# The end of the front of a two-layer macaron kernel: batch 0's score maxima in 1024-column units, ScalarE issuing two steps' transfers, and another order on SyncE's queue

## The reference, cut to what matters

```python
x = x + 0.5 * _L0_ffn_ref(_layernorm(x), W1, b1, W2, b2)
...
scores = jnp.einsum('bhqd,bhkd->bhqk', q, k) * scale
scores = jnp.where(causal, scores, -jnp.inf)
y_ar = jnp.einsum('bhqk,bhkd->bhqd', jax.nn.softmax(scores, axis=-1), v)
```

## Time and profile before

| what | value |
|---|---|
| time, median of 3 runs | 645.68 us (642.53 to 649.96) |
| profiled execution | 643.67 us |
| its span, first to last instruction | 641.9 us |
| PE busy | 521.5 us (81%) |
| DVE busy | 359.4 us (56%) |
| ACT busy | 197.0 us (31%) |
| POOL busy | 189.0 us (29%) |
| mean granted PE clock | 0.953 |

### The profile page before, as it was taken

How to read it: one execution, slowest core, us unless ns; L and a number is a source line. 1 busy time by engine, 2 the same in 40 slices (tenths; PEclk the granted TensorE clock), 3 DMA queues, 4 the chain that set the end, 5 groups by cost and what they waited for, 6 DMA issues and landing times.

```text
span 641.9 us, 10406 instructions
## 1 busy us (share of the span) xinstructions
PE 521.5 (81%) x3895; PEld 326.7 (51%) x3895; DVE 359.4 (56%) x942; ACT 197.0 (31%) x282; POOL 189.0 (29%) x228
## 2 busy tenths in 40 slices
PE   0788767999899989989877897894888878788893
PEld 0555333444544463445345773693345556663693
DVE  4753666466766767685044564132587888853131
ACT  0455331453154324424633450120223221110120
POOL 5676463010011102011110346654321212322163
PEclk9996798999999999999998997997998999988998
DMA  7317978732353244225269912323275455211320
GB/s 245 147 34 219 283 234 279 199 115 61 91 148 83 93 87 143 59 59 114 78 129 141 290 59 100 96 87 91 91 221 161 112 163 147 79 34 36 95 64 9
DMA packets 73666, 79.85 MB, mean 124 GB/s; under 512 B 10946, under 2 KB 50499, under 8 KB 73360
## 3 DMA queue, kind: packets, MB, share of 16 engines
q1 hardware_dynamic: 71056, 73.61, 41.4%
q0 software_dynamic: 2560, 5.58, 2.5%
HBM read 44.07 MB, written 35.72 MB: 124 GB/s over the span
## 4 chain that ended last, share of the span: by engine, by line
PE 49%; DVE 20%; issue 7%; DMA 6%; ACT 6%; POOL 5%; SPq 5%; POOLq 0%; DVEq 0%; ACTq 0%
PE ps_accum L1428 21%; PE ps_pair L1428 18%; PE ps_turn L1428 6%; DMA sb_ring<-sb_qs 3%; PE ps_turn L1436 2%; DVE sb_work L1178 2%; SPq L356 2%; POOL sb_rstd L569 2%; DVE sb_work L1323 2%; DVE sb_stats L1001 2%; DVE sb_mpart L1104 2%; SPq L350 1%; POOL xe_scr L589 1%; DMA sb_cols<-in_bias_cols 1%; PE ps_turn L1593 1%
## 5 line engine op out<-in xcount | busy, mean ns | idle before, releaser
L846 ACT ACTIVATE sb_work<-ps_pair 128x1024 f32<-128x1024 f32 x80 | 80.3, 1026 | 52.6 <-PE ps_pair L1428 51.8
L1104 DVE TENSOR_REDUCE sb_mpart<-ps_turn 128x4 f32<-128x512 f32 x80 | 55.0, 688 | 28.2 <-PE ps_turn L1428 28.1
L1428 PE MATMUL ps_pair<-sb_ring,sb_xsets 128*128 128x512 f32 x160 | 62.3, 465 | 6.7 <-ACT sb_work L846 3.5
L1104 DVE TENSOR_REDUCE sb_mpart<-ps_accum 128x4 f32<-128x512 f32 x80 | 55.0, 688 | 19.1 <-PE ps_accum L1428 18.3
L1428 PE MATMUL ps_pair<-sb_ident_bf,sb_ones_bf 128*128 128x512 bf16 x189 | 52.5, 437 | 12.1 <-DMA sb_x<-y_scr 7.8
L1428 PE MATMUL ps_accum<-sb_work,sb_v_aug 128*32 128x128 f32 (+3 forms) x768 | 53.9, 393 | 0.3 <-ACT sb_work L846 0.3
L1428 PE MATMUL ps_turn<-sb_ring,sb_m_sets 128*128 128x512 f32 x80 | 38.1, 477 | 9.4 <-DVE sb_mpart L1104 9.2
L567 POOL TENSOR_SCALAR sb_ve<-sb_mv 128x4 f32<-128x4 f32 x24 | 5.5, 228 | 133.5 <-DVE sb_mv L1004 126.9
L1428 PE MATMUL ps_accum<-sb_ring,sb_m_sets 128*128 128x512 f32 x80 | 40.6, 507 | 4.4 <-DVE sb_mpart L1104 3.8
L650 POOL TENSOR_TENSOR sb_e_pad<-sb_v_next,sb_y_ar 128x128 f32<-128x128 f32 x16 | 7.4, 460 | 122.8 <-DVE sb_y_ar L1148 122.8
L1428 PEld LDWEIGHTS ps_pair<-sb_ident_bf,sb_ones_bf 128*128 128x128 bf16 x189 | 20.4, 110 | 37.5 <-issue 13.2
(11 more groups left out here) (251 smaller groups left out, 991.3 us busy)
## 6 DMA issues: line engine op xcount, KB each, us to landing
sb_expert_rows<-xe_scr SPq DMA_DIRECT2D x16, 258.0 KB, 2.8
sb_m_sets<-q_scr SPq DMA_DIRECT2D x16, 256.0 KB
sb_xsets<-k_scr SPq DMA_DIRECT2D x16, 256.0 KB
sb_ka_stk<-mk_scr SPq DMA_DIRECT2D x4, 1024.0 KB
xe_scr<-sb_cst SPq DMA_DIRECT2D x4, 1024.0 KB, 12.8
sb_mw<-in_mw SPq DMA_DIRECT2D x16, 256.0 KB, 6.1
sb_ka_stk<-mk_scr SPq DMA_DIRECT2D x8, 512.0 KB
q_scr<-sb_qs SPq DMA_DIRECT2D x12, 256.0 KB, 3.4
```

Source lines behind the costliest of these rows:

```text
L846: act.activation(banks[:, 2 * i:2 * i + 2], pair[u % 2][:], ACT.Exp, scale=SCALE).then_inc(s["exp_done"], 1)
L1104: dve.tensor_reduce(mpart[:, m // NPAIR, m % NPAIR, :], max_banks[m % 2][:].rearrange("p (h k) -> p h k", h=HL), AX.X, ALU.max).then_inc(s ...
L1428: return pe.matmul(dst, lhsT, rhs, start=start, stop=stop, skip_group_check=True)
```

## The change

It has five parts.

1. The PSUM banks are declared anew: the two narrow banks become the halves of one double bank `max_pair`, and `wide_banks` are `pair[0]` and `max_pair`. `turn[1]` and `accum[1]` are now names for those halves.
2. Units 12 to 39 of batch 0 are done two at a time: `wide_scores` on PE fills both halves and signals once, `wide_maxima` on DVE reduces 1024 columns in one instruction. DVE's casts for batch 3 stand behind unit 17, no more behind unit 15.
3. ACT issues batch 0's first exponentials' set itself (`first_exp_set`), then loads the table of Exp, then does `max_t`, then issues the first row of maxima.
4. SP no longer issues those six transfers. Its order is now: `keep_features(3)`, batch 1's first maxima set, the second exponentials' set, the values, the second row.
5. `stay_awake` before the attention has 8 matmuls for 12.

```diff
--- before.py
+++ after.py
@@ -129,9 +129,11 @@
 
 
         pair = [psum(f"pair{i}", [P, 2, 512]) for i in range(2)]
-        accum = [psum(f"accum{i}", [P, 512]) for i in range(2)]
-        turn = [psum(f"turn{i}", [P, 512]) for i in range(2)]
-        max_banks = [turn[1], accum[1]]
+        max_pair = psum("max_pair", [P, 2, 512])
+        max_banks = [max_pair[:, i] for i in range(2)]
+        wide_banks = [pair[0][:], max_pair[:]]
+        accum = [psum("accum0", [P, 512]), max_banks[1]]
+        turn = [psum("turn0", [P, 512]), max_banks[0]]
 
         cst = sb("cst", [P, CONSTS.shape[1]])
 
@@ -438,17 +440,15 @@
             next_max_set(0, 1)
             keep_softmax(3)
             keep_features(3)
-            hold(sp, s["ffn_h"], NF * B)
-            for hs in range(2):
-                load_exp_set(0, hs)
-            hold(sp, s["v_kept"], 16 * B)
-            load_values(0)
             for kept in ("q_kept", "k_kept"):
                 hold(sp, s[kept], 48 * B)
             next_max_set(0, 2)
+            hold(sp, s["ffn_h"], NF * B)
+            load_exp_set(0, 1)
+            hold(sp, s["v_kept"], 16 * B)
+            load_values(0)
             hold(sp, s["max_t_evac"], 1)
-            for hs in range(2):
-                max_row(0, hs)
+            max_row(0, 1)
             next_max_set(0, 3)
             for kept in ("mq_kept", "mk_kept"):
                 hold(sp, s[kept], 48 * B)
@@ -829,6 +829,16 @@
                     act.wait_ge(s["q_kept"], 48 * B)
                 act.copy(mT, turn[1][0:H, :]).then_inc(s["max_t_evac"], 1)
 
+            def first_exp_set():
+
+                act.wait_ge(s["pad_zero"], 80)
+                act.wait_ge(s["q_kept"], 48)
+                act.wait_ge(s["k_kept"], 48)
+                for hl in range(HL):
+                    act.dma_start(ring[VW * hl:VW * hl + 3 * HD, 0, hl].bitcast(F32),
+                                  head_rows(q_scr, 0, hl, 3 * HD)).then_inc(s["xset0"], 16)
+                act.dma_start(x_sets[:, 0].bitcast(F32), set_rows(k_scr, 0, 0)).then_inc(s["xset0"], 16)
+
             def answers_out(b, hs):
 
                 act.wait_ge(s["pv_mm"], STEPS * b + NT * hs + NT)
@@ -877,8 +887,11 @@
             projections(B - 1)
             features(B - 1)
             keys_in_tokens(B - 1)
+            first_exp_set()
+            ready(ACT.Exp)
             max_t(0)
-            ready(ACT.Exp)
+            act.wait_ge(s["max_t_evac"], 1)
+            act.dma_start(ring[3 * HD:3 * HD + 1, 0].bitcast(F32), mT[0:HL].bitcast(F32)).then_inc(s["xset0"], 16)
             act.wait_ge(s["mq_kept"], 48 * B)
             act.wait_ge(s["mk_kept"], 48 * B)
             for b in range(B):
@@ -1104,6 +1117,15 @@
                     dve.tensor_reduce(mpart[:, m // NPAIR, m % NPAIR, :],
                                       max_banks[m % 2][:].rearrange("p (h k) -> p h k", h=HL),
                                       AX.X, ALU.max).then_inc(s["smax_red"], 1)
+
+            def wide_maxima(first, last):
+
+                for m in range(first, last, 2):
+                    hs, i = m // NPAIR, m % NPAIR
+                    dve.wait_ge(s["smax_mm"], m + 2)
+                    dve.tensor_reduce(mpart[:, hs, i:i + 2, :].rearrange("p i h -> p (i h)"),
+                                      wide_banks[m // 2 % 2].rearrange("p i (h k) -> p (i h) k", h=HL),
+                                      AX.X, ALU.max).then_inc(s["smax_red"], 2)
 
             def max_of_tiles(b):
 
@@ -1245,11 +1267,11 @@
             normalise(norm_first(3), x[3], xn_first[3], norm_first(3) % 2)
             for b in range(1, B):
                 before_attention(b)
-            maxima(0, 12, 16)
+            wide_maxima(12, 18)
             split(B - 1, 0)
             split(B - 1, 1)
             query_features(B - 1)
-            maxima(0, 16, NM)
+            wide_maxima(18, NM)
             max_of_tiles(0)
             for b in range(B):
                 attention(b)
@@ -1552,6 +1574,21 @@
                         last = mm(dst, ident_bf[:], bc(add_q_bf[:], HL), start=False)
                     last.then_inc(s["smax_mm"], 1)
 
+            def wide_scores(first, last_m):
+
+                for m in range(first, last_m, 2):
+                    hs = m // NPAIR
+                    if m % NPAIR == 0:
+                        pe.wait_ge(s[f"mset{hs % 2}"], 80 * (hs // 2 + 1))
+                    pe.wait_ge(s["smax_red"], m - 2)
+                    for a in range(2):
+                        qt, kt = MAX_PAIRS[m % NPAIR + a]
+                        dst = wide_banks[m // 2 % 2][:, a]
+                        last = mm(dst, tile(m_sets[:, hs % 2], qt), ring[:, 2 + hs % 2, :, kt * P:(kt + 1) * P], stop=qt != kt)
+                        if qt == kt:
+                            last = mm(dst, ident_bf[:], bc(add_q_bf[:], HL), start=False)
+                    last.then_inc(s["smax_mm"], 2)
+
             def max_turn(b):
                 pe.wait_ge(s["smax_red"], (NM + NT) * (b + 1))
                 for t in range(NT):
@@ -1700,21 +1737,21 @@
             pe.wait_ge(s["consts_bf"], 5)
             for b in range(B):
                 before_attention(b)
-            max_scores(0, 12, 16)
+            wide_scores(12, 16)
             turn_keys(B - 2)
             pe.wait_ge(s["ka_tok"], B - 1)
             turn_second(B - 1, values_of[(B - 1) % 2])
-            max_scores(0, 16, 18)
+            wide_scores(16, 18)
             project(B - 1)
-            max_scores(0, 18, 20)
+            wide_scores(18, 20)
             turn_keys(B - 1)
-            max_scores(0, 20, NM)
+            wide_scores(20, NM)
             max_turn(0)
             pe.wait_ge(s["proj_evac"], 2 * B)
             pe.wait_ge(s["ma_k"], B)
             pe.wait_ge(s["ffn_x"], B)
             pe.wait_ge(s["ka_tok"], B)
-            stay_awake(12, pair[1][:, 1])
+            stay_awake(8, pair[1][:, 1])
             pe.wait_ge(s["max_t_evac"], 1)
             for b in range(B):
                 attention(b)
```

## The result

Measured in 20 runs of each, the changed kernel takes 0.9949 of the time before (95% interval 0.9926 to 0.9971): medians 643.95 and 647.29 us, so 3.3 us less (1.9 to 4.8). The prediction was made against a median of 645.68; taken from there, the ratio gives 642.4 us, where 640.1 was forecast. The forecast was 5.6 us less. The time lies in the range, and "within 1%" was the likeliest case, but the gain is six tenths of the one forecast, and the interval does not reach it.

What follows compares the result with a forecast made beforehand. The attention's start was taken as the bound: first the row of maxima, then the values. Of the maxima's 7.0 us, 1.4 go unused, leaving 5.6 off the median 645.68: 640.1 us, range 637.2 to 644.6 for 8 in 10.

Steps and rivals of the forecast that it cites:

- within 1%: Case that the measured time differs from the time before by no more than 1%, 6.5 us; chance 0.68.
- Earlier casts: Batch 2's keys, the projection and DVE's casts come 1.15 us earlier, with units 16/17 reduced in the idle time ahead.
- Wide reductions: On DVE, 1.18 us per 1024-column reduction; the maxima's reductions end at 102.4 instead of 107.73, 5.3 us earlier.
- The set that this needs: SP issues maxima set 3 for unit 30 at 89.95 instead of 92.68, 2.7 us earlier; it lands at 95.
- The first row of maxima: ACT issues it at about 104.7; 3.14 us later, at 107.8, the attention's first matmul starts, 7.0 us earlier.
- The values: Now the late side: v_aug ready at 110.8 to 112.4, PE's third pair 4.5 to 6.1 us earlier, taken as 5.6.
- Stay awake and the clock: Eight idle matmuls before the attention take 3.5 us, 103.9 to 107.4; cost nothing if the clock is back by then.
- The rival: The clock: PE at half clock for 6.5 us around the attention's start costs 3.1 us, giving 643.2; chance 0.15.
- Nothing behind it absorbs the gain: Behind the attention's start every wait is on earlier work, so the 5 to 6 us gained there reach the end.

Runs made afterwards that it cites:

- x7: The changed kernel itself, run again beside the others: 0.9942 of the time before.
- x8: The changed kernel with 12 idle matmuls instead of 8 ahead of the first scores: 0.994 of the time before.
- x10: x9 with batch 0's maxima one unit at a time again: 1.0054 of the time before.
- x11: Changed kernel, batch 0's state loads and a maxima set moved behind the third exponentials' set, next batch's values ahead of the state: 1.0012 of before.
- x3: The changed kernel with batch 0's maxima one unit at a time again: 0.9993 of the time before.
- x2: The changed kernel with the values loaded ahead of batch 1's maxima set and the second exponentials' set: 0.9957 of the time before.
- x9: x12's kernel with batch 0's state loads, and a maxima set, moved behind the third exponentials' set: 0.9967 of the time before.
- x12: x2 with the next batch's values issued behind the fourth exponentials' set, second run of this kernel: 0.9927 of the time before.
- z2: The same kernel as x12, third run: 0.9897 of the time before.
- x4: The kernel before with only the new banks and wide units, ACT issuing nothing and SP's old order: 0.9961 of the time before.
- z1: The changed kernel with 10 idle matmuls in PE's wait for the values: 0.9922 of the time before.
- z3: The changed kernel itself, run a third time: 0.9936 of the time before.
- x1: The changed kernel with 16 idle matmuls in PE's wait for the values: 0.9932 of the time before.

## Why the prediction was right and wrong

**Earlier casts: right.** Batch 3's query features come 10.87 us behind the reference row instead of 12.13, 1.26 us earlier (forecast 1.15), and the reduction of units 16/17 fits in ahead of them.

**Wide reductions: right.** 1.22 us each, 1.17 apart (1.18), and DVE done 5.5 us earlier (5.3).

**The set that this needs: right.** SP loads maxima set 3 at 87.60, 12.1 us behind the reference row, not 14.9: 2.8 us earlier (2.7), with no wait for it.

**The first row of maxima: too dear.** From ACT's issue to the first matmul it took 2.43 us, not 3.14. That ACT's queue was empty does not explain it: in the other profiles where the row bounds the first pair and ACT issues it, it took 2.3 to 2.9 us in x7, x8, x10 and x11, but 3.0 to 4.0 in x3, and in x2, x9, x12 and z2, where the values go out just ahead of it. The transposes ran at full clock, 0.60 us against 1.02, which gives another 0.4. The first pair came 8.3 us earlier, not 7.0. This was worth nothing, since the values were later.

**The values: right in kind, 0.8 us too good.** They were to be the late side, and PE's row at 109.90 says so in as many words. The third pair came 34.4 us behind the reference row, 33.6 forecast. The values went out inside the bracket (29.5 us; 28.4 to 30.0), and POOL's copy began 4.2 us later (3.9). I had taken the early side of the middle: 5.6 us of 4.5 to 6.1, where 4.8 came. The Trainium skill ("DMA: Bandwidth & Descriptors", section "Issuing engines are not separate DMA queues") has transfers from all issuing engines interleave on the same 16 DMA engines. The traces agree, as far as one execution each can: beside ACT's set the twelve stores took 10.3 us of issue, from 89.83 to 100.11, where they took 9.8. That is 0.5 us, less than the 1.6 that I had worked out from the bytes. The better comparison is x4, with the same early start and no set on ACT: there the twelve took 9.05 us, which makes it 1.2, one execution each.

**Stay awake and the clock: the step that failed.** I wrote "I put the cost at nothing if the clock is back by then", and gave the fall of the clock a chance of 0.15. The condition looked at the eight matmuls ahead of the scores; they were harmless (x8). The idle time that I had myself forecast, PE waiting for v_aug, was the place. It was 2.6 to 5.2 us long, and the clock fell in it or at its end in all four profiles without idle matmuls there, with 8 or 12 ahead of the scores. z1 prices it: 1.5 us against z3, 2.7 against the first profile of the changed kernel. The term should have stood in the sum: 4.8 less some 2.3, the mean over the four profiles (11.8 us from third pair to copy 1 against 9.57), is 2.5 us, inside the interval of the measured 3.3 (1.9 to 4.8). This sum is made afterwards. In the runs' times the cost is not shown: with the wait filled, x1 and z1 have 0.9932 and 0.9922, without, the four results lie from 0.9936 to 0.9949, about 1 us more and within the noise. The rival had the right size, 3.1 us for one stretch, and the wrong chance.

**"Nothing behind it absorbs the gain": half wrong.** It is true for the changed kernel, whose copies 1 and 2 keep their distance of 11.0 us. But it held by little. Once copy 1 is over 2 us earlier still (x2, x12, z1, z2), the third exponentials' set is late. What is behind is not only waits on earlier work of the same kind: SP's order puts each exponentials' set behind a maxima set that has a wait of its own, and the state's loads, 2.0 MB where I had put "1.5 MB and more", are a block of about 10 us on the DMA engines. How the two share the lateness in x9 and x11 was not taken apart.

What stays open is how the missing 2.3 us (5.6 forecast, 3.3 measured) divide. The profiles give 0.8 to the values and 1.5 to 2.7 to the clock, measured at the start of the attention; the 3.3 rest on the time of whole runs.

## What to carry to other kernels

When a change leaves one engine waiting in a new place, price the wait twice: once as time, and once as a clock that has fallen when the work starts again. Idle matmuls belong where the new wait is, and short enough not to overrun it. Two halves of a change that end in the same place, here a faster producer and a shorter queue behind it, may each measure as nothing alone. And when a transfer is late in a queue with a hand-written order, look first at what stands ahead of it and what that waits for, and only then at the load on the engines; an edit that moves both at once can't tell them apart.

## What the runs showed of the hardware

One instruction that issues 256 KB held its sequencer 8.2 us right behind the state's loads, 2.0 MB issued in the 3 us before it, and 0.39 us behind a set of 448 KB (the two rows of SP's values). In the ten profiles with that order it was 7.4 to 8.6 us. On ACT, too, the issues stand in the engine's order: its five loads ran from 90.67 to 94.94, 4.3 us, where SP needed about 2.2 for the like, and the table load that comes next in its program began at 94.97. ACT was idle there, so it cost nothing.

The state's loads moved few bytes while the DMA engines were nearly full: 129 GB/s at a share of 1.07 at 115 us, against 389 at 1.06 at 98 us, where the stores and set loads ran (stretches of the changed kernel, here with the busy shares of PE, its weight loads, DVE, ACT and POOL). Which of the two kinds of transfer makes the difference, their rows or their direction, no run here tells:

```profile
98.00:99.00 1.00, 0.60 (x3) 0.10 (x1) 1.00 (x2) 0.00 (x0) 1.00 (x1) 1.00 1.06 389
```
